# The order in which the tiles of a perceiver layer are placed in SBUF, changed so that the loop's large tiles start at multiples of 256 bytes

## The reference

```python
x = x + _L0_xattn_ref(_layernorm(x), ctx_1024, ...)   # 16 heads of 64, 128 queries, 12544 keys
x = x + _L0_attn_ref(_layernorm(x), ...)              # self-attention, 16 heads of 16, with LoRA weights
x = x + _L0_ffn_ref(_layernorm(x), ...)               # one 256 x 256 linear map, rows and weights in fp8
```

```python
lat = layernorm(latents, ln_l_w, ln_l_b); ctx = layernorm(context, ln_c_w, ln_c_b)
q = lat @ Wq;  k, v = split(ctx @ Wkv)                # cut into 16 heads of 64
attn = softmax(clip(q k^T / 8, -11, 11));  out = attn v
return out @ Wo + bo
```

## Time and profile before

| | |
|---|---|
| median of three runs | 1185.73 us |
| lowest and highest | 1182.51 and 1188.33 us |
| the profiled execution | 1188.72 us |
| its span, first to last instruction | 1187.0 us |
| TensorE matmul busy | 1167.3 us (98%), 5056 instructions |
| TensorE weight load busy | 940.3 us (79%) |
| VectorE busy | 825.6 us (70%) |
| ScalarE busy | 598.0 us (50%) |
| GpSimd busy | 307.6 us (26%) |
| mean granted TensorE clock | 0.98 of full speed |

### The profile page before, as it was taken

How to read it: one execution, slowest core, us unless ns; L and a number is a source line. 1 busy time by engine, 2 the same in 40 slices (tenths; PEclk the granted TensorE clock), 3 DMA queues, 4 the chain that set the end, 5 groups by cost and what they waited for, 6 DMA issues and landing times.

```text
span 1187.0 us, 18331 instructions
## 1 busy us (share of the span) xinstructions
PE 1167.3 (98%) x5056; PEld 940.3 (79%) x5056; DVE 825.6 (70%) x1622; ACT 598.0 (50%) x1029; POOL 307.6 (26%) x516
## 2 busy tenths in 40 slices
PE   6999999999999999999999999999999999999997
PEld 5888888888888888888888888888888888888775
DVE  5777777777777777787776676676676676676532
ACT  4555555555555555555555555555555555555411
POOL 4333333333333333332121121121121121121000
PEclk8999999999999999999999999999999999999985
DMA  5221121221221221343221221211211211220000
GB/s 173 67 67 45 66 66 45 66 66 45 66 66 45 66 66 44 133 78 79 72 57 55 66 60 51 66 59 52 66 57 53 66 56 54 67 58 10 1 1 5
DMA packets 81393, 70.72 MB, mean 60 GB/s; under 512 B 40115, under 2 KB 67670, under 8 KB 81366
## 3 DMA queue, kind: packets, MB, share of 16 engines
q1 hardware_dynamic: 80390, 68.94, 19.6%
q10 hardware_dynamic: 976, 1.45, 0.4%
HBM read 70.13 MB, written 0.13 MB: 59 GB/s over the span
## 4 chain that ended last, share of the span: by engine, by line
PE 95%; issue 2%; DVE 1%; DMA 1%; POOL 0%; SPq 0%; ACT 0%; POOLq 0%; DVEq 0%; ACTq 0%
PE bank L467 31%; PE bank L468 31%; PE bank L466 31%; PE bank L511 1%; DMA wkT<-in_WkT_dram 1%; PE bank L572 1%; PE bank L584 1%; PE bank L614 0%; PE bank L596 0%; PE bank L503 0%; DVE fold_junk L913 0%; PE bank L630 0%; PE bank L594 0%; POOL wkT L457 0%; DVE fold_y L909 0%
## 5 line engine op out<-in xcount | busy, mean ns | idle before, releaser
L732 ACT ACTIVATE ex<-bank,c_rstd 128x512 f32<-128x512 f32 x392 | 269.7, 688 | 275.3 <-PE bank L468 262.3
L403 POOL TENSOR_TENSOR z_lo<-z,z_hi 128x255 fp32r<-128x255 f32 x196 | 173.8, 887 | 766.2 <-ACT z_hi L745 766.2
L739 ACT CAST p_hi<-ex 128x512 fp32r<-128x512 f32 x392 | 243.6, 621 | 234.7 <-DVE ex L899 161.3
L903 DVE TENSOR_TENSOR p_lo<-ex,p_hi 128x512 fp32r<-128x512 f32 x392 | 271.1, 692 | 116.6 <-ACT p_hi L739 99.8
L899 DVE TENSOR_SCALAR ex<-ex 128x512 f32<-128x512 f32 x392 | 186.7, 476 | 185.2 <-ACT ex L732 178.0
L468 PE MATMUL bank<-qk_hi,d_lo 128*128 128x512 f32 x784 | 310.3, 396 | 0.0
L466 PE MATMUL bank<-qk_hi,d_hi 128*128 128x512 f32 x784 | 310.2, 396 | 0.0
L467 PE MATMUL bank<-qk_lo,d_hi 128*128 128x512 f32 x784 | 310.1, 396 | 0.0
L468 PE MATMUL bank<-p_hi,z_lo 128*128 128x512 f32 x784 | 308.9, 394 | 0.0
L467 PE MATMUL bank<-p_lo,z_hi 128*128 128x512 f32 x784 | 308.5, 393 | 0.0
L466 PE MATMUL bank<-p_hi,z_hi 128*128 128x512 f32 x784 | 306.1, 390 | 0.0
(11 more groups left out here) (162 smaller groups left out, 420.2 us busy)
## 6 DMA issues: line engine op xcount, KB each, us to landing
t_all<-in_ctxT_dram SPq DMA_DIRECT2D x98, 384.0 KB, 3.2
x_pair<-in_ctx_dram SPq DMA_DIRECT2D x98, 256.0 KB, 2.7
diff<-sig_all SPq DMA_DIRECT2D x194, 0.5 KB, 1.9
wq<-in_Wq_dram ACTq DMA_DIRECT2D x2, 512.0 KB, 6.9
wkT<-in_WkT_dram SPq DMA_DIRECT2D x2, 512.0 KB, 6.1
wv<-in_Wv_dram SPq DMA_DIRECT2D x1, 1024.0 KB
wo<-in_Wo_dram SPq DMA_DIRECT2D x1, 1024.0 KB
crow_all<-in_crows_dram ACTq DMA_DIRECT2D x1, 256.0 KB, 7.6
```

What stands on the lines that cost most here:

```text
L403: pool.tensor_tensor(z_lo[s][:, b, 0:LAST], z[s][:, b, 0:LAST], z_hi[s][:, b, 0:LAST].bitcast(F32), ALU.subtract).then_inc(s_zlo, 1)
L732: act.activation(ex[c][:, :], sc_bank[c][:, :], ACT.Exp, scale=c_rstd[s4][:, b:b + 1])\
L739: act.copy(p_hi[b][c][:, :], ex[c][:, :]).then_inc(s_phi, 1)
L903: dve.tensor_tensor(p_lo[b][c][:, :], ex[c][:, :], p_hi[b][c][:, :].bitcast(F32), ALU.subtract)\
```

## The change

The declarations of lines 71 to 142 are put in another order. A pad of 128 bytes comes first, so that the next tile starts at 16640, a multiple of 256. Then come all tiles whose size is a multiple of 256 bytes per partition, and behind them the small ones. Shapes, types and names are the same. No instruction is added, taken out or moved on any engine, and no loop or wait is touched.

```diff
+        align_pad = sb("align_pad", [P, 32])
         ident = sb("ident", [P, P])
-        identb = sb("identb", [P, P], BF16)
-        ones_row = sb("ones_row", [1, P])
-        ... (last_row, neg_half, half_pow, warm, head_mask)
         x_sb = sb("x_sb", [P, D])
-        col_all = sb("col_all", [P, 6 * KD])
         crow_all = sb("crow_all", [P, 2, D])
         lat = sb("lat", [P, D])
-        stats, mv, veps, rstd
         latT ... wkE
-        neg_mean = sb("neg_mean", [P, MI])
         fold_junk, fold_y, qT, qk_hi, qk_lo, x_pair, t_all
-        c_stats, c_mv, c_rstd, c_veps, mean_all, rstd_all, sig_all
         z, diff, z_hi, z_lo, d_hi, d_lo, ex, p_hi, p_lo, sums, foldT
+        a_k1, f_bytes, f_w, f_wT, wv, wo, aw, f_b
+        identb, ones_row, last_row, neg_half, half_pow, warm, head_mask, col_all, stats, mv, veps, rstd,
+        neg_mean, c_stats, c_mv, c_rstd, c_veps, mean_all, rstd_all, sig_all
         neg_w_last, av, recip ...
```

More of the change, by code:

```diff
@@ L68, in perceiver_layer @@
         tr_bank = bank[6:8]
+        align_pad = sb("align_pad", [P, 32])
         ident = sb("ident", [P, P])
-        identb = sb("identb", [P, P], BF16)
-        ones_row = sb("ones_row", [1, P])
[L74 to L77, removed]
         x_sb = sb("x_sb", [P, D])
-        col_all = sb("col_all", [P, 6 * KD])
-        lat_w, lat_b, ctx_w, ctx_b, abq_col, abk_col = (col_all[:, n * KD:(n + 1) * KD] for n in range(6))
         crow_all = sb("crow_all", [P, 2, D])
@@ L84, in perceiver_layer @@
         lat = sb("lat", [P, D])
[L85 to L88, removed]
         latT = sb("latT", [P, KD, P])
@@ L102, in perceiver_layer @@
         t_pair = [t_all[:, s, :, :] for s in range(SLOTS)]
[L103 to L107, removed]
         z, diff = ([sb(f"{n}{s}", [P, 2, D]) for s in range(2)] for n in ("z", "diff"))
@@ L115, in perceiver_layer @@
         foldT = sb("foldT", [P, KD, D])
+        a_k1 = sb("a_k1", [P, P])
+        f_bytes = sb("f_bytes", [P, KD, D], U8)
+        f_w = sb("f_w", [P, KD, D], BF16)
+        f_wT = sb("f_wT", [P, KD, D], BF16)
+        wv = sb("wv", [P, KD, INNER])
+        wo = sb("wo", [P, MI, D])
+        aw = [sb(f"aw{n}", [P, KD, D]) for n in "qkvo"]
+        f_b = sb("f_b", [P, D])
+        identb = sb("identb", [P, P], BF16)
+        ones_row = sb("ones_row", [1, P])
+        last_row = sb("last_row", [P, 1])
+        neg_half, half_pow = sb("neg_half", [P, 2]), sb("half_pow", [P, 2])
+        warm = sb("warm", [P, 1])
+        head_mask = sb("head_mask", [P, HT])
+        col_all = sb("col_all", [P, 6 * KD])
+        lat_w, lat_b, ctx_w, ctx_b, abq_col, abk_col = (col_all[:, n * KD:(n + 1) * KD] for n in range(6))
+        stats = sb("stats", [P, 6])
+        mv = sb("mv", [P, 2])
+        veps = sb("veps", [P, 1])
+        rstd = sb("rstd", [P, 1])
+        neg_mean = sb("neg_mean", [P, MI])
+        c_stats = [sb(f"c_stats{b}", [P, 6]) for b in range(2)]
+        c_mv = [sb(f"c_mv{s}", [P, 2, 2]) for s in range(SLOTS)]
+        c_rstd = [sb(f"c_rstd{s}", [P, 2]) for s in range(SLOTS)]
+        c_veps = [sb(f"c_veps{s}", [P, 2]) for s in range(2)]
+        mean_all, rstd_all, sig_all = (sb(n, [P, TILES]) for n in ("mean_all", "rstd_all", "sig_all"))
         neg_w_last = sb("neg_w_last", [P, 1])
@@ L118, in perceiver_layer @@
         recip = sb("recip", [P, H])
-        a_k1 = sb("a_k1", [P, P])
         a_max = sb("a_max", [P, AH])
@@ L128, in perceiver_layer @@
         f_qT = sb("f_qT", [P, KD, P], BF16)
[L129 to L134, removed]
         bo_row = sb("bo_row", [1, D])
-        aw = [sb(f"aw{n}", [P, KD, D]) for n in "qkvo"]
         aa_all = sb("aa_all", [R, 4 * D])
@@ L140, in perceiver_layer @@
         abv_row, abo_row = sb("abv_row", [1, D]), sb("abo_row", [1, D])
-        f_b = sb("f_b", [P, D])
         wvE = sb("wvE", [P, KD, H, VW])
```

## The result

| | before | after |
|---|---|---|
| median | 1186.62 us | 1158.20 us |
| lowest and highest | 1182.51 and 1188.33 us | 1157.57 and 1160.53 us |
| ratio, with its 95% interval | | 0.9769 (0.9740 to 0.9799) |
| profiled execution, span | 1187.0 us | 1156.1 us |

Four runs of each stand behind it. The forecast was 1185.7 us with a range from 1177 to 1194, so the time fell well outside.

What follows compares the result with a forecast made beforehand. TensorE, busy without a gap in the loop, was taken to bound the kernel. Every term was 0, so the profiled 1188.7 us stayed, carried to a median of 1185.7 us, range 1177 to 1194.

Steps and rivals of the forecast that it cites:

- What bounds the kernel: Whole span: TensorE, never held up in the loop, sets the time; 1 ns of matmul distance is worth 4.7 us.
- The moving operand: Loop matmuls: aligning the streamed operand changes nothing; 0 taken, between bounds of -7.1 and +7.1 us.
- The weights: Loop weight loads: 188 to 190 ns at three different placements, beside the running matmul; 0 taken.
- The rule on lines: SBUF reads: only crossing 16-byte lines costs, so any multiple of 32 bytes is as good; loop term exactly 0.
- The bounds for the whole loop: All 4704 matmuls: if placement causes uneven steps, 22.6 us less or 24.5 us more; 0 taken.
- The third: Rival, whole loop: alignment removes the unevenness, all steps come to 226.7 ns; -22.6 us, 1163 us; 6%.
- The first: Rival, qk matmuls: weights and moving operand at equal offsets by 256 help, 3.0 ns each; -7.1 us, 1178.6 us; 7%.
- The second: Rival, sum blocks: aligned moving operands p_hi and p_lo are slower, 3.0 ns each; +7.1 us, 1192.8 us; 6%.
- fourth: Rival, whole loop: reads at the same offset hinder each other, all steps 236.7 ns; +24.5 us, 1210 us; 5%.
- the estimate of 1111 us: All 4704 matmuls at the Trainium skill page's distance of 215.7 ns: 74 us less; no step that short in the rows.
- Other engines, transfers, start: VectorE, ScalarE, GpSimd, context loads and wkT's landing: each 0; the start at most 1.3 us either way.
- What would show it: Signs: 863 to 865 matmuls from 900 to 1100 us, unchanged group durations; wrong if means move 3 ns or more.

Runs made afterwards that it cites:

- e10: Changed kernel with z and p starting 96 bytes past a multiple of 256, d and qk at 0, so each matmul's operands agree: 1182.51 us, ratio 0.9982.
- e12: Changed kernel with z_lo alone moved to 96 bytes past a multiple of 256: 1177.27 us, ratio to before 0.9942.
- e7: Changed kernel with the weights' tiles (z, d) 32 bytes past a multiple of 256, moving operands at 0: 1191.33 us, ratio to before 1.0056.
- e4: Changed kernel with a first pad of 224 instead of 128 bytes, every large tile 96 bytes past a multiple of 256: 1161.11 us, ratio to before 0.9798.
- e9: Kernel before with qk_hi and qk_lo alone moved from 0 to 96 bytes past a multiple of 256, matching weights and p: 1162.82 us, ratio 0.9817.
- e1: Changed kernel with the weights' tiles (z, d) put back to 96 bytes past a multiple of 256, other large tiles at 0: 1196.05 us, ratio to before 1.0093.
- e16: Changed kernel with the weights' tiles cut from one tile, 4 bytes past a multiple of 256, moving operands at 0: 1187.03 us, ratio to before 1.0001.
- e17: Changed kernel with the weights' tiles cut from one tile at a multiple of 256, like the moving operands: 1160.01 us, ratio to before 0.9785.
- e6: Changed kernel with the weights' tiles 128 bytes past a multiple of 256, moving operands at 0: 1188.30 us, ratio to before 1.0017.

## Why the prediction was wrong

**What bounds the kernel: right.** TensorE held the end before and after, and nothing else took its place. That 1 ns of distance is worth 4.7 us held too: for 5.1 ns, start and loop together became 24.8 us shorter.

**The moving operand: the step that failed.** The loop's distance stood in the sum at 0 and gave -24 us. I read rows 3 as a comparison of an aligned (qk) with an unaligned operand (p), and bounded the price by their difference, 7.1 us. It wasn't a comparison of a disturbed with an undisturbed kind. Both were disturbed. The p blocks had equal rests but followed the qk blocks, whose rests were unequal, and e10 to e12 show that a difference disturbs its neighbours. Both kinds fell, qk from 396 to 390 or 389 and p from 394, 393 and 390 to 390, 389 and 390. The 3.0 ns that I took for the widest end were the difference of two losses, one of about 6 and one of about 3 ns.

**The weights: 0 was wrong in kind.** I looked at the duration of a load, 188 to 190 ns at any rest, which was true and stayed so. The cost isn't in the load; it is in the distance of the matmuls.

**The rule on lines.** The page "SBUF — State Buffer" of the Trainium skill ("Specifications (TRN2)") names lines of 16 bytes, and by it the loop's term was exactly 0. The runs don't bear that use of it out: a shift of the weights by 32 bytes, two whole lines, cost 6.6 ns a matmul in e7 against the changed kernel.

**The bounds for the whole loop: the size was there.** 226.7 ns, the shortest half block of the earlier trace rows, is the very pace after. I dismissed it because two halves of a p block with the same addresses took 0.70 and 0.68 us. The observation was right and the conclusion wrong: in this kernel the unevenness went with the disturbance, and it need not follow a matmul's own address.

**The rivals.** The third, every step at 226.7 ns, gave -22.6 us, and the loop gave -24; I had it at 6%. The first named the condition, equal rests, but for each matmul by itself, which e10 shows isn't enough, and priced it at the qk blocks alone, -7.1 us. The first's condition, widened to the whole stream, and the third's price are what happened. The second and fourth fell with e4 and e9. No run has a distance under 226.7 ns, so nothing here bears out the estimate of 1111 us.

**Other engines, transfers, start: right.** p_lo stayed at 693 ns. VectorE's d_lo rose from 686 to 710 ns, hidden. The first use of wkT waited 2.4 us in place of 1.3, within the 1.3 us allowed. The tail moved by 6.1 us, more than the 0.9 us allowed, by the clock.

**What would show it.** The means of qk moved by 6 ns, past the 3 ns that I had named as refuting me. The window from 900 to 1100 us, with 872 instructions, isn't a clean measure, since the changed kernel's loop ends in it.

## What to carry to other kernels

Where TensorE is busy without a gap but its steps differ in length for no visible reason, or are all longer than the shortest seen (in e1 all are), compare the places of all weights and moving operands of the stream, by 256 bytes. Here they had to agree with one another; that they be at multiples of 256 was not needed, and one pad of 96 bytes ahead of the odd tiles did what the reordering did. A comparison of two kinds of instruction inside one stream bounds nothing unless one of them is known to be undisturbed.

## What the runs showed of the hardware that wasn't expected

- The distance of fp32r matmuls of 512 columns with a weight load each was 226.7 ns with all rests equal, and 230.6 to 234.3 ns otherwise, at a granted clock of 1.00.
- A difference of 4 bytes between the weights' and the moving operands' places cost 5.7 ns a matmul (e16 against e17), one of 128 bytes 5.7 ns (e6 against the changed kernel).
- One tile at another rest (e12) slowed blocks that don't use it.
- One program had two times: 2 of 11 executions with a difference of 16 bytes took 1160 us, the others 1189 to 1194, at mean granted clocks that were alike (0.984; 0.982 to 0.988).
